# Decoder layer in float32: eight subtractions of the weight unpacking move from VectorE to GpSimd

## The reference, cut to what matters

```python
x = layernorm(x + attention(x))      # causal in chunks of 64, no softmax, 16 heads of 16
x = layernorm(x + long_conv(x, ctx)) # products of channel pairs, filtered by taps k
Wg, Wu, Wd = dequant(gate), dequant(up), dequant(down)
x = layernorm(x + (gelu(x @ Wg.T) * (x @ Wu.T)) @ Wd.T)
```

## Time and profile before

| what | value |
|---|---|
| median of three runs | 573.89 us |
| the profiled execution's own time | 574.71 us |
| its span, first to last instruction | 572.4 us |
| TensorE (PE) busy | 539.1 us, 94% |
| VectorE (DVE) busy | 375.3 us, 66% |
| ScalarE (ACT) busy | 148.0 us, 26% |
| GpSimd (POOL) busy | 123.3 us, 22% |
| mean granted TensorE clock | 0.98 of 2.4 GHz |

### The profile page before, as it was taken

How to read it: one execution, slowest core, us unless ns; L and a number is a source line. 1 busy time by engine, 2 the same in 40 slices (tenths; PEclk the granted TensorE clock), 3 DMA queues, 4 the chain that set the end, 5 groups by cost and what they waited for, 6 DMA issues and landing times.

```text
span 572.4 us, 9307 instructions
## 1 busy us (share of the span) xinstructions
PE 539.1 (94%) x3385; PEld 439.7 (77%) x3385; DVE 375.3 (66%) x782; ACT 148.0 (26%) x259; POOL 123.3 (22%) x195
## 2 busy tenths in 40 slices
PE   5999979989989999999999999999999997699993
PEld 5766757766878888776888888866888885588883
DVE  3998888975876577875455668875454778533334
ACT  3422200252333112232232111332333110222230
POOL 2100078210002445120003444120003451200001
PEclk9999899999999999999999999999999999599998
DMA  5532342130110110023001110040001110100001
GB/s 173 156 80 79 89 118 66 38 111 2 48 45 29 46 50 26 0 78 108 1 1 38 56 40 16 0 147 0 0 0 46 55 46 2 37 1 0 1 0 37
DMA packets 25249, 26.69 MB, mean 47 GB/s; under 512 B 2816, under 2 KB 22784, under 8 KB 25216
## 3 DMA queue, kind: packets, MB, share of 16 engines
q1 hardware_dynamic: 14208, 15.73, 9.3%
q10 hardware_dynamic: 10576, 8.95, 5.1%
q0 software_dynamic: 432, 1.57, 0.8%
HBM read 24.15 MB, written 2.10 MB: 46 GB/s over the span
## 4 chain that ended last, share of the span: by engine, by line
PE 82%; DVE 9%; DMA 3%; issue 2%; POOL 1%; ACT 1%; ACTq 0%; POOLq 0%; DVEq 0%; SPq 0%
PE bank L911 17%; PE bank L913 15%; PE bank L912 15%; PE front_bank L1030 5%; PE front_bank L1033 4%; PE front_bank L1031 4%; PE front_bank L972 4%; PE front_bank L959 3%; PE bank L906 3%; PE front_bank L911 2%; PE front_bank L912 2%; PE front_bank L913 2%; PE front_bank L1004 2%; DVE st L719 1%; DMA wo_sb<-in_woT 1%
## 5 line engine op out<-in xcount | busy, mean ns | idle before, releaser
L911 PE MATMUL bank<-x2T_lo,ffn_hi 128*128 128x512 f32 x256 | 111.6, 436 | 4.1 <-DVE x2T_lo L838 4.1
L854 DVE TENSOR_TENSOR inter<-bank,inter 128x512 f32<-128x512 f32 x64 | 44.2, 690 | 95.6 <-PE bank L913 95.3
L913 PE MATMUL bank<-x2T_hi,ffn_hi 128*128 128x512 f32 x256 | 102.2, 399 | 0.0
L912 PE MATMUL bank<-x2T_hi,ffn_lo 128*128 128x512 f32 x256 | 101.9, 398 | 0.0
L436 POOL TENSOR_TENSOR qbd<-qT_sb,ctxT_sb 128x256 f32<-128x256 f32 x128 | 77.8, 631 | 76.8 <-PE front_bank L1033 63.3
L386 POOL TENSOR_TENSOR ve<-ve,minus_half 128x2 f32<-128x2 f32 x24 | 17.4, 743 | 301.0 <-DVE ve L726 229.8
L911 PE MATMUL bank<-ffn_lo,inter_hi 128*128 128x256 f32 x256 | 77.2, 302 | 0.8 <-DVE inter_lo L848 0.8
L588 ACT ACTIVATE inter_hi<-inter 128x512 fp32r<-128x512 f32 x64 | 40.4, 632 | 143.0 <-DVE inter L854 143.0
L582 ACT ACTIVATE inter<-bank 128x512 f32<-128x512 f32 x64 | 38.2, 598 | 134.5 <-PE bank L913 134.5
L913 PE MATMUL bank<-ffn_hi,inter_hi 128*128 128x256 f32 x256 | 72.0, 281 | 0.0
L912 PE MATMUL bank<-ffn_hi,inter_lo 128*128 128x256 f32 x256 | 71.9, 281 | 0.0
(11 more groups left out here) (115 smaller groups left out, 795.3 us busy)
## 6 DMA issues: line engine op xcount, KB each, us to landing
toep_sb<-in_toep ACTq DMA_DIRECT2D x64, 128.0 KB, 2.1
xT_sb<-in_xT SPq DMA_DIRECT2D x4, 512.0 KB, 6.3
ctxT_sb<-in_ctxT SPq DMA_DIRECT2D x4, 512.0 KB, 4.4
x_sb<-in_x SPq DMA_DIRECT2D x4, 512.0 KB, 5.3
ctx_sb<-in_ctx SPq DMA_DIRECT2D x4, 512.0 KB, 6.3
out<-ctxT_sb POOLq DMA_DIRECT2D x3, 512.0 KB, 3.4
raw_w<-in_gate_p SPq DMA_DIRECT2D x8, 128.0 KB
raw_s<-in_gate_s SPq DMA_DIRECT2D x8, 128.0 KB
```

What stands on the lines that cost most here:

```text
L854: nc.vector.tensor_tensor(inter[:, n % 2, :], up_ps[:, :], inter[:, n % 2, :], ALU.mult).then_inc(inter_ready, 1)
L911: nc.tensor.matmul(ps, w_hi, x_lo, start=start, stop=False, skip_group_check=True)
L912: nc.tensor.matmul(ps, w_lo, x_hi, start=False, stop=False, skip_group_check=True)
L913: return nc.tensor.matmul(ps, w_hi, x_hi, start=False, stop=stop, skip_group_check=True)
```

## The change

GpSimd gets an `unpack` of its own. It computes the low parts of pieces 4 to 11, each in the score step one after the piece was scaled: it waits until the scores of that step are done and until ScalarE has rounded the piece. VectorE leaves these eight out; the waits on low parts count two semaphores instead of one. In the first group ScalarE spreads all queries (that of step 1 in the turn, right behind that of step 0). A score step has 5 unread products in place of 8.

```diff
+        FIRST_SCORE = START + 4
+        def with_mask(q):
+            return FIRST_SCORE <= q + 1 < FIRST_SCORE + NU_S
+        def low_parts(eng, k):
+            beside_masks = sum(with_mask(q) for q in range(k))
+            if k > beside_masks:
+                eng.wait_ge(wlo_ready, k - beside_masks)
+            if beside_masks:
+                eng.wait_ge(wlo_pool, beside_masks)
...
             def score(g, u):
-                if u + 2 < NU_S and u % 2:
+                if u + 2 < NU_S and u % 2 and not (isinstance(g, int) and g == 0):
                     spread(g, u + 2)
+            def unpack(step):
+                q = step - 1
+                if with_mask(q):
+                    m, c = units[q]
+                    pool.wait_ge(s_mm, step - FIRST_SCORE + 1)
+                    pool.wait_ge(whi_ready, q + 1)
+                    nc.gpsimd.tensor_tensor(ffn_lo[:, m, :, c * QC:(c + 1) * QC], weight[:, q % 2],
+                                            ffn_hi[:, m, :, c * QC:(c + 1) * QC].bitcast(F32), ALU.subtract)\
+                        .then_inc(wlo_pool, 1)
...
-                    spread(g, 1)
+                    if not isinstance(g, int) or g:
+                        spread(g, 1)
...
-                last.then_inc(spread_ready[0], 1)
+                last.then_inc(spread_ready[u % 2], 1)
...
-                if u + 2 < NU_S and u % 2 == 0:
+                if u + 2 < NU_S and (u % 2 == 0 or isinstance(g, int) and g == 0):
                     spread(g, u + 2)
...
                     spread(g, 0)
+                    if isinstance(g, int) and g == 0:
+                        spread(g, 1)
                     vproj(g, 0)
...
-                if 0 <= q < NU:
+                if 0 <= q < NU and not with_mask(q):
...
                     if n >= 2:
-                        dve.wait_ge(wlo_ready, n - 1)
+                        low_parts(dve, n - 1)
...
-                keep_busy(g, 8 if u < NU_S else 4)
+                keep_busy(g, 5 if u < NU_S else 4)
...
-                    pe.wait_ge(wlo_ready, 3 * (n // 2) + m)
+                    low_parts(pe, 3 * (n // 2) + m)
```

More of the change, by code:

```diff
@@ L170, in decoder_layer @@
             "ms_ready", "newton_step", "rms_ready", "half_ready", "sk_ready", "x2lo_ready", "inter_ready", "ilo_ready")
-        shifted, masked, deq_ready, wlo_ready = sems("shifted", "masked", "deq_ready", "wlo_ready")
+        shifted, masked, deq_ready, wlo_ready, wlo_pool = sems("shifted", "masked", "deq_ready", "wlo_ready", "wlo_pool")
         y_ready, st_ready, mv_ready, ve_ready, ln_ready = (
@@ L449, in turn @@
                     pool.dma_start(out_v[:, bass.ds(at, NB), :], res_sb).then_inc(stored, 16)
-            schedule(pool, turn, {"score": score, "norm": norm, "x1T": x1T, "conv": conv}, nothing, nothing, nothing, nothing,
+            schedule(pool, turn, {"score": score, "norm": norm, "x1T": x1T, "conv": conv}, nothing, nothing, nothing, unpack,
                      lambda: rstd(G - 1, 2))
```

## The result

The changed kernel takes 581.5 us (median of six runs, 579.5 to 585.0), the kernel before 573.9 in the same series; the ratio is 1.0131, with an interval from 1.0107 to 1.0156. The forecast had the direction, and the mechanism in the score stage, but 575.8 us; the time lies above its range, 571.0 to 579.0. The profiled execution took 581.6 us against 574.71, with a span of 580.0 against 572.4.

The account below looks back on a forecast made before the run. TensorE and VectorE together bound the score step; held shifts make it 3.70 us. 0.39 + 2.36 - 0.6 - 0.25 = +1.9 on the profiled 574.71 gives 576.6; with the median 0.82 lower, 575.8 us, range 571.0 to 579.0.

Parts of the forecast that it names:

- Two engines carry the step together: First group's score steps: TensorE and VectorE together set the 3.30 us step, so both must get shorter.
- When GpSimd starts, and that it holds the shifts: Score steps: GpSimd starts 0.83 behind the scaling's end, subtracts for 1.27 and holds VectorE's shifts; step 3.70 us.
- First interval +0.39: First interval between causal masks: shifts go at 30.91 in place of 30.52, +0.39 us.
- six more +2.36: The six further intervals between causal masks: 22.20 in place of 19.84 us, +2.36.
- tail -0.6: Behind the eighth causal mask: fewer products stand before the last sums, which still need the mask; -0.6 us.
- Step 13, -0.25: Step 13 loses its low part, shifts to scaling 1.53 becomes 1.05; between 0 and -0.48, taken as -0.25 us.
- Rival 1, shifts not held: Score steps: shifts are not held and steps shorten to 2.81 to 3.14; 570.0 to 572.0 us, chance 0.20.
- Rival 3, the clock: Score stage: TensorE's granted clock falls; one half-clock step gives 577.1 us, all seven 585; chance 0.10.
- Later pieces and groups only shift: Everything after the first group's priced terms: it only moves in time, with no term in the sum.
- 5 not 8 products: TensorE in score steps: five products take 1.29 in place of 2.06 us, so its step would be 2.52.

Follow-up runs that it names:

- e2: The kernel before with 5 in place of 8 unread products a step and nothing else: 575.9 us (1.0027 of before).
- e3: The changed kernel with GpSimd's low part one score step later: 575.6 us (1.0020 of before).
- e8: The changed kernel with the second group's input load held until 13 filter products are done and 40 waits added to TensorE's program: 574.7 us (1.0004 of before).
- e7: The kernel before with the second group's input load held until 13 filter products are done: 572.5 us (0.9973 of before).
- e6: The kernel before with 5 unread products a step and 12 long-past waits per score step in place of the others: 573.9 us (0.9993 of before).
- e1: The changed kernel with 20 very short unread products added behind the score steps, restoring TensorE's program length: 578.0 us (1.0062 of before).
- e9: A second execution, unchanged, of the changed kernel with GpSimd's low part one score step later: 575.6 us.

## Why the prediction was right or wrong

- *Two engines carry the step together.* Half shown: e2 took products from TensorE alone, and the step stayed at 3.27. No run took the low part from VectorE alone; with both taken and nothing held (e3) it was 2.82, for 2.81 in the prediction.
- *When GpSimd starts, and that it holds the shifts.* Right: start 0.81 behind the scaling's end (32.92 to 33.73) for a forecast 0.83, subtraction 1.27 for 1.27, step 3.71 for 3.70, resumption 0.14 before GpSimd's end as in the earlier trace rows. By the Trainium skill ("SBUF — State Buffer", two separate sides), of a GpSimd operation and a VectorE operation that needs the ports both share, the one that starts first has them for its whole instruction and the other waits. These rows agree: shifts of 0.49 took 1.38 beside a subtraction that had started 0.24 earlier.
- *First interval +0.39, six more +2.36, tail -0.6.* Measured +0.41, +2.44 and -0.54. *Step 13, -0.25*: from the mean of squares to the residual sum 10.68 in place of 11.06, -0.38. These four make 1.93, for 1.9; that it is so close owes something to luck, since the terms were off by up to 0.13 in both directions. With the 0.24 by which this execution's first mask came earlier, 1.69 is left at the residual sum. e8 against e7 gives 1.8 to 2.2 in all.
- *Rival 1, shifts not held,* is false, as every step shows. *Rival 3, the clock,* did not come true where I put it: in the score stage the granted clock stayed at 1.00 though TensorE idled about 1.06 us a step. It fell in the convolution, behind the longer pause for a filter.
- *"Later pieces and groups only shift."* This is the step that failed, and it held two errors. First, the convolution: the load and the filters race each other. The load of the second group was issued 2.05 us behind the first filter product before (78.94 to 76.89), 1.47 now (80.03 to 78.56), and one filter fewer got ahead of it. This follows the kernel and not the execution: 2.06 and a pause of 1.4 to 1.5 in e2 and e6, 1.48 and 2.0 to 2.2 in e1, e3 and e9. The remedy is worth 1.8 in the kernel before and 3.2 in the changed one, so the change added some 1.4. Second, the program's length: "5 not 8 products" was priced as TensorE time alone, and the number of instructions ahead of the loop, on which its loading depends (e2, e6), was not priced. That is worth 3.5 (e1). With the hold's 2.2 these make 7.1 of the 7.6 measured; by the ratios to the kernel before in each series it is 4.0, 1.6 and 1.8, about 7.4 of 7.5.

In the range I left no room for either, because every bound in it came from the score stage.

What stays open: what brought the load 0.58 us forward. SyncE issues it right behind a fetch that waits for VectorE's scaling of piece 16, and that scaling ended 0.98 behind the first filter product before (77.87 to 76.89), 0.41 in the changed kernel (78.97 to 78.56):

```profile
76.72 1.15 DVE L654 SCALAR_TENSOR_TENSOR weight<-code,raw_s 128x512 f32<-128x512 f16 x1 [0.46 <-DVE code L650]
```

```profile
78.07 0.90 DVE L683 SCALAR_TENSOR_TENSOR weight<-code,raw_s 128x512 f32<-128x512 f16 x1
```

Before, the scaling stood 0.46 idle and then took 1.15 beside GpSimd's products; in the changed kernel it took 0.90. That two GpSimd products got ahead of it in one kernel and one in the other fits these times and was not tried apart. Nor was it tried at which lengths of TensorE's program the loop runs without loading. Of the changes of -0.3 and -0.95 around the other two turns, the first stands in every run with GpSimd's low part (27.2 in place of 27.5 to 27.6 us), and its cause is open; the last turn lies between 22.7 and 23.8 us in all runs, whatever the kernel.

## What to carry to other kernels

An operation moved to GpSimd must be timed by its last input, not by the wait that names the work it should hide under; if the input is made just before, one step of delay can turn a hold into an overlap. And when an edit changes the number of instructions ahead of a loop, look at the instruction packets and at pauses for issue around the loop's end before reading the rest of the difference as the edit's work.

## What the runs showed that I had not expected

Removing 24 products of TensorE that nothing reads, 48 instructions, made the kernel slower (e2, 575.9), and 48 instructions that only wait for what is long there made it as fast as before again (e6, 573.9). Instruction packets stood at 20 or 29, nothing between, and the turn at 27.2 to 27.3 us with 20 and at 29.7 to 31.8 with 29. A pause of 2.66 us for a filter was followed by 3 us of half clock in one execution, while pauses of 2.0 to 2.2 in others (e1, e3, e9) were not; the 16 filter products took 24.9 us there, 26.95 in the changed kernel's profile and 22.7 with the load held.
